# Attention with the Q projection spread over 13 of a head's 18 pairs, and both norms of a head's Q taken behind its second half

## The reference

```python
q = (x @ wq + bq).reshape(B, S, H, D)
scores = jnp.einsum('bqhgd,bkhd->bhgqk', q, k) * scale
scores = jnp.where(causal, jnp.float32(-1000000000.0), scores)
weights = jax.nn.softmax(scores, axis=-1)
out = jnp.einsum('bhgqk,bkhd->bqhgd', weights, v)
```

## Time and profile before

| what | us |
| --- | --- |
| median of 3 runs | 2820.11 |
| lowest and highest of the 3 | 2630.99, 2851.16 |
| the profiled execution | 2397.82 |
| its span on the slowest core (core 6) | 2396.3 |
| spans of the 8 cores | 2388.2 to 2396.3 |
| TensorE matmul busy | 2319.0 |
| VectorE busy | 824.9 |
| ScalarE busy | 621.6 |

### The profile page before, as it was taken

How to read it: one execution, slowest core, us unless ns; L and a number is a source line. 1 busy time by engine, 2 the same in 40 slices (tenths; PEclk the granted TensorE clock), 3 DMA queues, 4 the chain that set the end, 5 groups by cost and what they waited for, 6 DMA issues and landing times.

```text
span 2396.3 us, 32016 instructions; the slowest of 8 cores (2388.2 to 2396.3 us)
## 1 busy us (share of the span) xinstructions
PE 2319.0 (97%) x11140; PEld 1016.3 (42%) x11364; DVE 824.9 (34%) x1505; ACT 621.6 (26%) x789; POOL 78.6 (3%) x148
## 2 busy tenths in 40 slices
PE   5899999999999999999999999999999999999999
PEld 2344433333333443444444444444444444444444
DVE  2432245566554335323333332111333333333101
ACT  1444437777776332111111110000111111110000
POOL 2000000000000000000000000000000000000000
PEclk9999999999999999999999999999999999999999
DMA  9624111111355830522443237776223442234872
GB/s 160 104 36 71 18 27 19 19 19 27 66 84 107 193 112 1 100 52 51 84 84 61 45 57 140 163 165 148 50 53 65 84 79 47 48 74 85 184 158 89
DMA packets 57285, 193.46 MB, mean 81 GB/s; under 512 B 10246, under 2 KB 14854, under 8 KB 48940
## 3 DMA queue, kind: packets, MB, share of 16 engines
q0 software_dynamic: 23808, 139.99, 34.1%
q1 hardware_dynamic: 33324, 51.40, 6.7%
HBM read 306.18 MB, written 25.18 MB: 138 GB/s over the span
## 4 chain that ended last, share of the span: by engine, by line
PE 90%; DMA 3%; issue 2%; ACT 2%; DVE 1%; another core or an unknown queue 1%; POOL 0%; DVEq 0%; ACTq 0%; SPq 0%; POOLq 0%
PE pq L1275 32%; PE pq L1437 15%; PE pq L900 5%; PE pq L729 5%; PE pq L453 4%; PE pq L414 4%; PE pq L628 4%; PE pq L1302 4%; PE pq L1287 4%; PE pq L1353 4%; PE pq L781 4%; DMA wkv_wv<-wv_h 2%; PE pq L799 2%; DMA out_d<-dx_stg 1%; ACT wc_p L742 1%
## 5 line engine op out<-in xcount | busy, mean ns | idle before, releaser
L1275 PE MATMUL pq<-dv_xln,dw_wsl 128*128 128x512 bf16 x3513 | 804.7, 379 | 4.3 <-ACT ds_s L1320 0.3
L1275 PEld LDWEIGHTS pq<-dv_xln,dw_wsl 128*128 128x128 bf16 x3584 | 350.2, 98 | 424.5 <-issue 3.7
L1437 PE MATMUL pq<-dx_x2s,dw_wsl 128*128 128x512 bf16 x1754 | 388.4, 379 | 5.6 <-DVE dx_stg L1455 2.2
L1320 ACT ACTIVATE ds_s<-pq 128x512 bf16<-128x512 f32 x112 | 66.9, 597 | 939.1 <-PE pq L1302 884.3
L1337 DVE TENSOR_TENSOR ds_x<-ds_s,pq 128x512 bf16<-128x512 bf16 x108 | 74.3, 688 | 650.6 <-PE pq L1302 614.8
L742 ACT ACTIVATE wc_p<-pq,gl_nb 128x1024 bf16<-128x1024 f32 (+4 forms) x252 | 256.2, 1046 | 71.9 <-PE pq L729 65.6
L1437 PEld LDWEIGHTS pq<-dx_x2s,dw_wsl 128*128 128x128 bf16 x1792 | 174.7, 98 | 216.8 <-issue 7.2
L1455 DVE TENSOR_TENSOR dx_stg<-pq,dx_stg 128x512 f32<-128x512 f32 x64 | 42.0, 688 | 334.6 <-PE pq L1437 141.9
L781 PE MATMUL pq<-wc_p,pp_V 128*128 128x512 bf16 (+3 forms) x493 | 139.6, 363 | 1.1 <-DVE pl_p L753 0.2
L1287 PE MATMUL pq<-dp_c,dw_wsl 128*128 128x512 bf16 x438 | 131.1, 379 | 2.2 <-DVE dp_d L1098 1.7
L1302 PE MATMUL pq<-dp_d,dw_wsl 128*128 128x512 bf16 x440 | 131.3, 379 | 1.6 <-DVE xg_x L1328 1.0
(11 more groups left out here) (183 smaller groups left out, 1750.6 us busy)
## 6 DMA issues: line engine op xcount, KB each, us to landing
dw_wsl<-w_h POOLq DMA_DIRECT2D x56, 1216.0 KB, 10.0
dw_wsl<-w2b_h POOLq DMA_DIRECT2D x16, 960.0 KB, 10.8
dw_wsl<-w2a_h POOLq DMA_DIRECT2D x16, 896.0 KB, 9.6
wa_xr<-x_tiles POOLq DMA_DIRECT2D x6, 2048.0 KB, 40.2
wc_wq<-wq_h POOLq DMA_DIRECT2D x16, 512.0 KB, 5.7
dw_ev<-xo_oc SPq DMA_DIRECT2D x32, 256.0 KB, 6.1
wo_w<-wo_h POOLq DMA_DIRECT2D x16, 512.0 KB, 14.8
xres_d<-dw_ev SPq DMA_DIRECT2D x32, 256.0 KB, 6.1
```

Of the source, the lines that this page charges most:

```text
L1275: ms = [(lambda hc, bank=bank, wo_=wo_: (lambda e: e.matmul(bank[:, 0:TD], w[:, wo_ + hc * 128: wo_ + (hc + 1) * 128], xln2[tt][:, hc * TD ...
L1437: ms.append((lambda j=j, t=t: (lambda e: e.matmul(banks[t][:, 0:TD], w[:, j * 128:(j + 1) * 128], x2s[:, j * 2 * TD + t * TD: j * 2 * TD + ...
```

## The change

The squares get two buffers: `csq[0]` as before for half 0, and for half 1 the buffer `llo` of the row sums' split, which is not in use then. Half 1's projection waits only for half 0's evacuation (`q_ev[(g, 0)]`). The norm of half 0 moves from j 10 to j 17, behind the evacuation of half 1 (for which its matmul waits, as the bank is the same), and the norm of half 1, at j 0 of the next head, waits for half 0's maximum. `l_split` waits for the norm that still reads `llo`. The projection goes over the pairs 2 to 7 and 9 to 15, in groups of 2 and 3 matmuls, where it went over 3 to 7 and 12 to 15 in groups of 3 to 5. In head 0, the norm of head 1's second half moves from j 2 to j 1.

```diff
-        csq = WC.al('csq', [128, 512], BF16)
+        csq0 = WC.al('csq', [128, 512], BF16)
         lhi = WC.al('lhi', [128, 512], BF16)
         llo = WC.al('llo', [128, 512], BF16)
+        csq = [csq0, llo]
...
                 elif half == 1:
-                    wts.append(('ve', qn_ve[(g, 0)]))
+                    wts.append(('ve', q_ev[(g, 0)]))
...
             wts = [('ve', q_ev[(g, half)])]
-            if half == 1:
-                wts.append(('pe', qn_pe[(g, 0)]))
+            if g >= 2 and half == 1:
+                wts += [('pe', qn_pe[(g - 1, 1)])] + ([('pe', comb_rr[(g - 3, 'pe')])] if g >= 3 else [])
             elif g:
-                wts.append(('pe', qn_pe[(g - 1, 1)]))
+                wts.append(('pe', qn_pe[(g - 1, half)]))
             qsq_ve[(g, half)] = P.g('vector', [
-                lambda e: e.tensor_mul(csq, q_sb[g % 3][:, sl], q_sb[g % 3][:, sl]),
+                lambda e: e.tensor_mul(csq[half], q_sb[g % 3][:, sl], q_sb[g % 3][:, sl]),
             ], waits=wts, inc='ve')
...
             qn_pe[(g, half)] = P.g('tensor', [
-                lambda e: e.matmul(bank[:, 0:512], onb_sb, csq, start=True, stop=True,
+                lambda e: e.matmul(bank[:, 0:512], onb_sb, csq[half], start=True, stop=True,
                                    skip_group_check=True),
-            ], waits=[('ve', qsq_ve[(g, half)])], inc='pe')
+            ], waits=[('ve', qsq_ve[(g, half)])] + ([('ve', qn_ve[(g, 0)])] if half else [('ve', q_ev[(g, 1)])] if g >= 2 else []),
+                inc='pe')
...
                 lambda e: e.tensor_tensor(llo, b_l[:, 0:512], lhi, op=ALU.subtract),
-            ], waits=[('ve', v)], inc='ve')
+            ], waits=[('ve', v), ('pe', qn_pe[(min(h + 2, NH - 1), 1)])], inc='ve')
...
-        QA = {3: (0, 3), 4: (3, 6), 5: (6, 9), 6: (9, 12), 7: (12, 16)}
-        QB = {12: (0, 3), 13: (3, 7), 14: (7, 11), 15: (11, 16)}
+        QA = {2: (0, 3), 3: (3, 6), 4: (6, 9), 5: (9, 12), 6: (12, 14), 7: (14, 16)}
+        QB = {9: (0, 2), 10: (2, 4), 11: (4, 6), 12: (6, 8), 13: (8, 11), 14: (11, 13), 15: (13, 16)}
...
-                    if j == 10:
+                    if j == 17:
                         q_norm(g, 0)
...
-                if h + 1 < NH and j == (0 if h else 2):
+                if h + 1 < NH and j == (0 if h else 1):
                     q_norm(h + 1, 1)
```

## The result

The changed kernel takes 2404.74 us in the median of 7 runs, the kernel before 2396.84 us in the median of its 7. In some executions of this program, whatever the kernel, the cores of a die show a lower clock and the time is longer (in the changed kernel's run of 2801.79 us four cores show 0.835 to 0.837 and the others 0.996 to 0.997; in all runs of the first four experiments cores 4 to 7 show about 0.98 or less), and the ratios leave such runs out. The ratio is 1.0037, 95% interval 1.0027 to 1.0047: slower, by 0.4% (8.7 us between the means), clear of noise and far inside 2%. The predicted time, 2830.5, is wrong: the three runs shown for before (2630.99 to 2851.16) lie far above the four taken later (2394.76 to 2396.84), which are next to the profiled execution (2397.82). The forecast made against that execution was 2408.2, or 0.43% more.

A forecast was written before the change was run, and what follows sets the result against it. TensorE was taken to bound the kernel, with short bubbles; 0.91 less 0.22 per head over 14 heads, plus 0.75 for head 0, made 10.4 us, put on the median 2820.11: 2830.5 us, range 2640 to 2864.

The forecast's parts named there:

- the last of the sum: Adding the 10.4 us to the shown median of 2820.11 instead of the profiled 2397.82, giving 2830.5 us.
- The rival with a slower TensorE: TensorE's work stretched about 1.18 in timed runs: loss 0.42 us per head, time 2826.8 us; chance 0.20.
- The second norm's wait: TensorE waits at the next head's pair 0 for the first half's maximum, behind pair 13's accumulation: 0.91 us per head.
- S16: The scores matmuls of pair 16; VectorE was forecast free for the maximum 2.57 us after them.
- S0: Bubble before the next head's pair 0 scores falls from 0.39 to 0.17 us, a norm matmul entering pair 17.
- S9: New bubble of 0.20 us before pair 9's scores, as pair 7 has two Q matmuls fewer.
- S10: Bubble before pair 10's scores becomes 0.24 us, from 0.44; pair 9 now has two Q matmuls.
- the 1.62 us from E7 to E8: Pair 8's exponential begins 1.62 us after pair 7's, two small activations of the bound lying between.
- Head 0: Head 1's second norm at pair 1 queues pair 2's scores behind it: 0.75 us once, from 0 to 3.5.
- Waits taken as nothing: Q matmuls at pairs 2, 10, 11, the second half's evacuation wait and the row-sum split's wait: 0 us.
- The wait is hidden: First maximum ends early enough that the second norm never waits: 2817.8 us, or 2811.6; chance 0.17.
- The low clock spreads: Head 0's longer gap and later gaps bring half-rate TensorE stretches: +16 to +25 us, 2836 to 2845; chance 0.06.

The follow-up runs named there:

- the first four experiments: The changed kernel with, one each: pair 13's accumulation behind the first maximum; Q matmuls at old pairs; that maximum taken twice; head 0 as before. No time ratios.
- head0_back: The changed kernel with head 0's Q matmuls and second norm placed as before; no time ratio, attention 429.7 us against 430.4.
- defer_acc: The changed kernel with pair 13's accumulation queued on VectorE behind the first norm's maximum; no time ratio, attention 420.3 us against 430.4.
- two_maxima: The changed kernel with the first norm's maximum taken twice in a row on VectorE; no time ratio, attention 438.6 us against 430.4.
- spread_first_half: The kernel before with only the first half's Q matmuls over pairs 2 to 7 and head 1's second norm at pair 1 of head 0; ratio 1.0032.
- second_norm_at_pair1: The changed kernel with the second norm at pair 1, first half's Q matmuls in pairs 3 to 7, head 0 as before; ratio 0.9970 against before.

## Why the prediction was right or wrong

**The stated time: wrong.** The step that failed is the last of the sum, putting the 10.4 us on the median shown, 2820.11. Its text saw that all three runs lay far above the profiled execution and took them for the kernel's time; the runs that count for before lie at 2394.76 to 2396.84. The range, 2640 to 2864, rested on the same reading and falls with it. The rival with a slower TensorE fails as to the time, as the cores compared have TensorE at 1.00 in the attention; what the change costs at a lower clock, its 0.42 per head, was not measured. The rule of the current limit in the Trainium skill ("TensorE: Matmul & The Clock Gate", section "Seeing it yourself"), by which three cores of a die with dense matmuls are enough to lower its clock, isn't borne out in the profiled execution of the changed kernel: TensorE is busy for 97% of the span on all eight cores, and their mean clock is 0.996 to 0.998. A lower level is on record all the same, for a few us at a time: core 6 of head0_back shows 0.81 from 158.5 to 165.5 us and 1.00 from 166 to 191.

**The difference: right in sign, place and mechanism of its largest term,** +0.37% against +0.43% forecast: 8.7 us between the means of the runs and 8.4 in the attention, for a forecast of 10.4. Term by term, per head:

- The second norm's wait: forecast 0.91, measured 0.97. The maximum begins 2.64 us after S16, not 2.57, because the square starts 0.99 behind the evacuation where it was 0.92. defer_acc and two_maxima show the cause.
- S0: forecast 0.39 to 0.17, measured the same.
- S9: forecast 0.20, measured 0.22.
- S10: forecast 0.24, measured 0.04. This is the term that was mis-sized: 0.20 per head, 2.8 us in all. I took the 1.62 us from E7 to E8 for a fixed cost of the small activations. In the changed kernel the distance is 1.44 (501.81 to 503.25), and in spread_first_half too; where pair 7 has four Q matmuls again (second_norm_at_pair1) it is 1.62. With E8 0.18 earlier, pair 9's two Q matmuls nearly close the bubble: S9 and S10 together have 0.26 in place of 0.44, where I had them unchanged. A reason can be argued from the earlier trace rows: S8 begins at 500.85 and E8 at 501.60, 0.75 later, which is the plain distance from scores to exponential (0.76 from S7 to E7), so that E8 was waiting for its scores. It doesn't cover the odd heads: there the distance fell by the same 0.18, from 1.90 to 1.72, though S8 begins 1.03 before E8 in the kernel before. The size is shown, the reason stays open.
- Head 0: forecast 0.75, measured roughly 0.7.
- Waits taken as nothing: right in the changed kernel, but the wait at pair 2's first Q matmul was hidden only by the norm's. It is 0.14 and 0.26 where that one is gone.

**The rivals.** "The wait is hidden" fell, but its version exists: with the second norm one pair later it is what happens, and the time falls below before's. "The low clock spreads" fell: the clock is at 1.00 in every later head of the changed kernel, with a wait of 0.97 us in each that projects.

## What to carry to other kernels

When two steps are moved next to each other on one bank, the price is the consumer's round trip, and that includes whatever the in-order engine has queued ahead of the consumer: read that queue, not only the consumer's duration. Filling bubbles with spread work pays where a chain is longer than the work beside it, and costs where the work taken away was covering one. And before a sum is put on a median, ask whether the profiled execution and the timed runs show the same time: 2397.82 beside 2820.11 was a reason to give the sum on the profiled one.

## What the runs showed that I had not expected

Cores 0 to 3 of one kernel repeat their pitch to 0.01 or 0.02 us, and two kernels with the same steady part, traced apart, have the same (the changed kernel and head0_back: 27.02 and 27.30), so a change of 0.1 us per head is visible in one trace, while the timed ratio has an interval of 0.2%. An alternation of 0.28 us between heads goes with E8 and is in every kernel; what causes it stays open.
